# Moving the newest head's counts to the front of ScalarE's step, with the counts buffer held twice

## What is computed

```python
dots = jnp.einsum('bhij,hk->bkij', dots, pre_proj)
dots = jnp.where(causal[None, None], neg, dots)
top = lax.top_k(dots, SPARSE_TOPK)[0]
dots = jnp.where(dots < top[..., -1:], neg, dots)
attn = jax.nn.softmax(dots, axis=-1)
attn = jnp.einsum('bhij,hk->bkij', attn, post_proj)
```

## Time and profile before

| | |
|---|---|
| time, median of 3 runs | 3607.39 us (3606.74 to 3607.62) |
| the profiled execution's own time | 3610.26 us |
| its span | 3608.5 us |
| ACT busy | 3177.0 us (88%) |
| DVE busy | 2962.0 us (82%) |
| PE busy | 2833.9 us (79%) |
| POOL busy | 2009.9 us (56%) |
| granted TensorE clock, mean | 0.881 |

### The profile page before, as it was taken

How to read it: one execution, slowest core, us unless ns; L and a number is a source line. 1 busy time by engine, 2 the same in 40 slices (tenths; PEclk the granted TensorE clock), 3 DMA queues, 4 the chain that set the end, 5 groups by cost and what they waited for, 6 DMA issues and landing times. The chain is left out here.

```text
span 3608.5 us, 70619 instructions
## 1 busy us (share of the span) xinstructions
PE 2833.9 (79%) x13751; PEld 1830.1 (51%) x13751; DVE 2962.0 (82%) x12236; ACT 3177.0 (88%) x9018; POOL 2009.9 (56%) x3687
## 2 busy tenths in 40 slices
PE   7788787878868887788878768877787888777765
PEld 3455555555545555555555545555455555555544
DVE  4588888888888888888888888888888888888883
ACT  1799999999979999999999979998899999999982
POOL 3355655555555565655655545564655555565544
PEclk9888989898988988888998988988898898989876
DMA  1000000000000000000000000000000000000000
GB/s 41 7 2 2 5 8 5 8 2 5 8 4 8 5 2 8 5 8 5 8 2 5 8 4 8 5 8 2 5 8 5 8 5 2 8 5 8 2 7 4
DMA packets 31403, 22.65 MB, mean 6 GB/s; under 512 B 3201, under 2 KB 30338, under 8 KB 30722
## 3 DMA queue, kind: packets, MB, share of 16 engines
q1 hardware_dynamic: 30722, 16.03, 1.6%
HBM read 11.83 MB, written 4.19 MB: 4 GB/s over the span
## 5 line engine op out<-in xcount | busy, mean ns | idle before, releaser
L881 ACT ACTIVATE signs<-scores,state 128x528 int8<-128x528 f32 (+3 forms) x3072 | 1760.0, 573 | 199.5 <-DVE state L1102 106.6
L1276 POOL TENSOR_SCALAR probs<-probs,rinv 128x528 f32<-128x528 f32 (+3 forms) x1024 | 541.4, 549 | 1416.3 <-DVE rinv L1132 1415.3
L747 PE MATMUL t_bank<-ident,probs 128*128 128x128 f32 x2560 | 519.4, 329 | 590.1 <-POOL probs L1276 540.8
L1284 POOL TENSOR_TENSOR work<-scores,work 128x528 f32<-128x528 f32 (+3 forms) x1024 | 887.6, 903 | 15.8 <-DVE work L1024 15.8
L723 PE MATMUL s_bank<-xn,gT 128*128 128x512 f32 (+3 forms) x2048 | 800.0, 515 | 9.5 <-ACT gT L813 6.8
L734 PEld LDWEIGHTS y_bank<-u_all,probsT 128*128 128x128 f32 x5120 | 631.3, 197 | 135.5 <-issue 122.6
L747 PEld LDWEIGHTS t_bank<-ident,probs 128*128 128x128 f32 x2560 | 312.0, 160 | 712.3 <-issue 554.9
L734 PE MATMUL y_bank<-u_all,probsT 128*128 128x128 f32 x5120 | 636.9, 281 | 7.8 <-ACT probsT L892 7.7
L1127 DVE SCALAR_TENSOR_TENSOR probs<-scores,kth,expo 128x528 f32<-128x528 f32 (+3 forms) x1024 | 521.9, 564 | 82.4 <-issue 70.9
L881 ACT ACTIVATION_READ_ACCUMULATOR signs<-scores,state 128x1 f32 x3072 | 573.8, 187 | 0.0
L1024 DVE TENSOR_SCALAR_CACHE_REDUCE work<-scores,state 128x528 f32<-128x528 f32 (+3 forms) x1024 | 527.6, 553 | 46.6 <-DVE state L1102 41.4
(11 more groups left out here) (148 smaller groups left out, 3240.2 us busy)
## 6 DMA issues: line engine op xcount, KB each, us to landing
xwork<-in_L_attn_x_dram SPq DMA_DIRECT2D x17, 256.0 KB, 2.9
xres<-in_L_attn_x_dram SPq DMA_DIRECT2D x16, 256.0 KB, 3.0
out_dram<-ybuf SPq DMA_DIRECT2D x16, 256.0 KB, 2.4
u_all<-in_L_attn_Wq_dram SPq DMA_DIRECT2D x1, 512.0 KB, 3.8
u_all<-in_L_attn_Wk_dram SPq DMA_DIRECT2D x1, 512.0 KB, 4.6
u_all<-in_L_attn_Wv_dram SPq DMA_DIRECT2D x1, 512.0 KB, 5.4
u_all<-in_L_attn_Wo_dram SPq DMA_DIRECT2D x1, 512.0 KB
expo<-in_L_ffn_w_gate_dram SPq DMA_DIRECT2D x1, 192.0 KB, 4.8
```

The costliest lines, as they stand in the source:

```text
L747: mm = nc.tensor.transpose(t_bank[q % 2][:, at:at + P], probs[:, h % 2, KEY_AT[t] + j * P:KEY_AT[t] + (j + 1) * P], ident[:, :])
L881: nc.scalar.activation(signs[:, k, 0:ROW[t]], row(scores, ring(head_of(s, k + 1), RING), t), ACT.Sign, bias=guesses(s % STATES, k, GUESSES ...
L1276: nc.gpsimd.tensor_scalar(prb, prb, rinv[:, slot_p, t:t + 1], 1.0, ALU.mult, ALU.mult).then_inc(scaled, 1)
L1284: nc.gpsimd.tensor_tensor(wrk, row(scores, slot_k, t), wrk, ALU.subtract).then_inc(hidden, 1)
```

## The change

`counts` gets a second half, picked by the parity of the step: ScalarE writes half `s % 2`, and the move reads half `(s - 1) % 2`, the one of the step before. ScalarE's step now begins with `count(0)`. The first of the four exponentials comes ahead of `take_turned(2)`, and `take_extra(1)` behind it. No instruction's work is changed, and none is added but two or three register instructions.

```diff
-        counts = sb("counts", [P, GUESSES * T])
+        counts = sb("counts", [P, 2, GUESSES * T])
...
-                                                 accum_out=counts[:, k * T + t:k * T + t + 1]
+                                                 accum_out=counts[:, s % 2, k * T + t:k * T + t + 1]
                                                  ).then_inc(counted[k], 1)
...
+                    count(0)
                     count(2)
                     if s == LAG_V and kind != "first":
...
                     take_turned(1)
-                    count(0)
+                    exponentials(0)
+                    take_turned(2)
                     take_extra(1)
-                    take_turned(2)
-                    for p in range(T):
+                    for p in range(1, T):
                         exponentials(p)
...
-                        v.tensor_tensor(miss, counts[:, :], aim_sum, ALU.subtract).then_inc(guess_step, 1)
+                        v.tensor_tensor(miss, counts[:, (s - 1) % 2, :], aim_sum, ALU.subtract).then_inc(guess_step, 1)
```

More of the change, by code:

```diff
@@ L1217, in _ @@
             nc.gpsimd.memset(state[:, :], 0.0).then_inc(state_set, 1)
-            nc.gpsimd.memset(counts[:, :], 0.0).then_inc(state_set, 1)
+            nc.gpsimd.memset(counts[:, :, :], 0.0).then_inc(state_set, 1)
             pool.wait_ge(state_set, 2)
```

## The result

The changed kernel takes 3658.7 us (median of 4 runs, 3656.14 to 3663.43), the kernel before 3607.06 on the same chip: a ratio of 1.0146, 95% interval [1.0128, 1.0163]. It is 52 us slower. I had forecast 16 us slower; the direction and the mechanism hold, and the size is off by a factor of three. One execution of the kernel under "The product last, `count(0)` in the middle" was in a slower state (3681 us at a granted clock of 0.687), and the ratio there leaves it out.

A forecast was written before the change was run, and what follows sets the result against it. ScalarE was busiest, with 123 us of waits in a ring with VectorE. Gains of 36.5 us against costs of 53 made +16 us on 3610.3, or 3626; the runs' median lies 2.9 lower, so 3623 us, range 3572 to 3660.

The forecast's parts named there:

- Moved counts, two halves: ScalarE's waits for the move fall from 123 to 60 to 80 us; VectorE's wait for counts nears zero.
- Places: Middle batch: gain 0 at steps 7 to 9, 1.5 us at 15 to 2, 0.3 at 13; 27 us in all.
- gain 0: Steps 7 to 9: ScalarE's work on that stretch is the same set, so its 0.17 + 2.40 us of waits stay.
- The first batch: Five waits, 7.5 us in sum, against some 0.7 us of new wait in each of four steps: gain 4.5 us.
- the missed guesses: Five of ScalarE's waits for PE, with VectorE on the long way: gain 1 us each, 5 us.
- The second extra product: Its cover falls from 3.08 to 1.30 us, against 1.18 needed at full clock, 2.13 at the lower: cost 53 us.
- How often: Share of second extra products made at the lower clock: 0.58, taken as 0.45 us of mean wait.
- Who pays: Steps 2, 3 and 13 pay 1.35 us, 9 to 12 1.5, step 14 0.7: 3.5 us a batch, 53 us.
- vanish: Steps 8, 15, 0 and 1: product waits lie in chains that VectorE bounds and disappear in its waits.
- The products stay fast: Rival, chance 0.26: PE gets the full clock at the second extra product; 5 us of cost against 36.5, 3576 us.
- The whole ring: Rival, chance 0.05: MAX8 does not wait for `flags`, so the 123 us of waits go; 3535 us at best.
- no first activation waited for the masking: Rival, chance 0.03: `count(0)` at the head of ScalarE's step waits for VectorE's masking; 1 us in a third of steps, 3690 us.

The follow-up runs named there:

- The product last, `count(0)` in the middle: Kernel before the change, with only the copy of the second extra product moved behind the exponentials: 3607.05 us, ratio 0.9999.
- the kernel with the product last: Changed kernel, with the copy of the second extra product moved behind the last exponential: 3573.78 us, ratio 0.9911 to the kernel before.
- the old tail: Changed kernel, with the rest of ScalarE's step in the old order (second extra product, small transposed copy, four exponentials): 3790.21 us, ratio 1.0506.

## Why the prediction was off in size

*Moved counts, two halves.* Right. VectorE's waits for the counts are near zero (11.3 us, and 10.5 to 13.5 in the variants), the halves cost nothing, and the copy of `flags` is what VectorE now waits for, 248.9 us in 164 places. ScalarE's waits for the move fell to 52.7 us; I had said 60 to 80. Of them 38.5 are at steps 8 and 9, as forecast.

*Places.* Steps 7 and 8, in which the waits of steps 8 and 9 fall, take 28.9 us before and after; "gain 0" was right. Steps 15, 0 and 1 fell by 0.7 us (table above) and not by 1.5. The sum let the products' waits of these steps, and of step 8, vanish in those that VectorE causes there. In step 8 they do so, 11.3 us of them, and steps 6 to 8 are no longer than before. In steps 15, 0 and 1 they do not: they are 28.6 us in 15 batches. In the kernel with the product last, where they are gone, the same steps are 1.7 us shorter than before, close to the forecast. The first batch, from its first copy of `gT` to that of the next batch, is 2.9 us shorter and not 4.5. What the missed guesses gave was not taken apart.

*The second extra product.* The price was right and the count wrong. For a slow product I had 0.83 us, and the steps show 0.86. The step that failed is **"How often"**, the 0.45 us in the mean, together with the terms built on it under **"Who pays"**: the 0.7 us for step 14 and the "vanish" for steps 15, 0 and 1. I took the share of slow products from the mean of a row for all products, 0.58. Counted off in the timelines behind the first batch, the second products other than those of steps 6, 7 and 14 end more than 1.4 us behind the copy of `gT` in 116 of 164 cases before the change (0.71) and in 127 of 164 after it (0.77). So the share was wrong for the kernel before already. In the seven steps that were to pay, 2, 3 and 9 to 13, it did not change (72 of 105, then 73): that PE's work stays as sparse holds there. Elsewhere it does not hold. In steps 0 and 1 the product is slow in 15 of 15 batches each, where it was in 14 and 8. In step 14 it ends some 2.98 us behind the copy in all 15, before in 5, and 2.8 us behind it in 2 more.

By the table a batch pays 3.15 us in steps 2, 3 and 9 to 13, where the sum had 2.55 (2.85 less the 0.3 won at step 13), and 1.7 us in step 14, where it had 0.7. With the 0.8 us missing in steps 15, 0 and 1 and 0.4 won in steps 6 to 8, that is 2.0 us a batch, 30 of the missing 36 us. The first batch has 1.6 more.

*Rivals.* "The products stay fast" was said to need PE's transposes earlier in the step, and did not come. Whether the new gap ahead of the flags matmul, which I had named against it, is the reason is not shown. The early transposes alone do not lower the clock: with the product copied last they are as early, and the granted clock is 0.878 to 0.887 as before the change (0.878 to 0.885). Among the kernels with VectorE's order as it was, it is lowest where ScalarE waits most for the products: 0.868 to 0.872 in the changed kernel, 0.852 to 0.856 with the old tail. That fits waits that lengthen PE's pauses and so make more products slow, but no run tests it by itself. The whole ring did not go, and no first activation waited for the masking.

*The page on the clock.* By "TensorE: Matmul & The Clock Gate" of the Trainium skill, section "HAM oscillation — how this bites in real kernels", a long unbroken gap would be behind the fall. The trace does not agree: here the clock fell behind a stretch with PE busy 1.45 of 3.50 us, with no idle time above 1.66 us. The measurement decides. Doubling short transposes raised the granted clock of the run from 0.868 to 0.928, and moving one copy in the kernel before raised it from 0.88 to 0.914. So in this kernel the level goes with how PE's work is spread; by what rule is not shown.

## What to carry to other kernels

When an instruction is moved away from a place, list what it covered there: `count(0)` hid one wait of the engine it ran on, and that wait was worth more than the one the move removed. Price the uncovered wait at the slower of the two TensorE clocks, and count the slow cases among the very instructions concerned, step by step. The mean of a group hides them (0.58 against a counted 0.71), and the change itself can add to them, as it did in step 14. When a reordering loses, look for the second-order fix before undoing it: the same change with one copy placed last is 0.9% faster than the kernel before.

## What was not expected of the hardware

More work on PE made other PE work faster: with 2048 transposes more, the 512 value matmuls fell from 368.9 to 294.7 us. And a wait on ScalarE costs about 0.1 us more than its idle time shows (0.86 against 0.76 us), because copies that follow each other without a wait overlap by that much (the small copy ends at 1831.19, and `u_all` starts at 1831.08).
